# A twelve-layer network on one core: passes of two products, zeros, gathers and products of ones

## The chip, the cores and the metric

The kernel runs on one core of a Trainium2 chip. The core has a matrix engine (TensorE, PE in the profile), VectorE (DVE), ScalarE (ACT), GpSimd (POOL) and SyncE (SP), which share an on-chip memory of 128 partitions; PE writes its results to eight banks of PSUM. The metric is the device time of one execution in microseconds (us).

## The reference

`x` is 2 x 512 tokens of 256 features. Twelve sublayers are added to it, each on a layernorm of `x`. The change touches the expert layers (`_L2_ffn_ref`, two of them), the attention between them (`_L2_attn_ref`) and the waits around the last three (`_L3_ffn_ref` on both sides of `_L3_attn_ref`).

```
# L2 attention: 16 heads of 16 features, causal, each batch on its own
q, k, v = split_heads(x @ Wq.T + bq), split_heads(x @ Wk.T + bk), split_heads(x @ Wv.T + bv)
attn = softmax(where(causal, -inf, einsum('bhqd,bhkd->bhqk', q, k) * scale))
ctx  = einsum('bhqk,bhkd->bhqd', attn, v)
return ctx.reshape(b, t, D) @ Wo.T + bo

# L2 experts: 8 experts of 176 hidden features, two per token, and a shared one of 352
topk_scores, topk_idx = top_k(softmax(x @ Wr.T), 2)
out_e = einsum('bsef,edf->bsed', silu(x @ Wg[e].T) * (x @ Wu[e].T), Wd)
return sum over the two chosen experts(out_e * score) + shared

# L3 ffn: x @ (weights of -1, 0 or 1).T + bias
```

## The kernel before, in words

The work is cut into 24 units: unit u is sublayer u // 2 on batch u % 2. Each engine runs its own list of instructions and waits on semaphores where it needs another. Units 12 and 13 are the first expert layer, 14 and 15 the attention (16 heads each), 16 and 17 the second expert layer, 18 and 19 an L3 ffn, 20 and 21 the L3 attention, 22 and 23 the last ffn.

**Passes.** Values are float32. A factor is split into a high part, rounded to what one pass of PE takes (fp32r), and a low part, the rest. `mm3` (L291 to L293) makes a product of two split factors from three passes: high x high, high x low, low x high. `mm3c` does so for each chunk of 128 rows of the sum. In the profile L291, L292 and L293 are these three passes wherever `mm3` is called.

**Expert tiles** (`pe_moe2`, `act_moe2`, `dve_moe2`). GpSimd scatters the tokens to DRAM by expert. They come back in tiles of 128 tokens, 15 per batch, so 30 per layer, each with one expert whose place in `m_a` (high) and `m_b` (low) is read into a register (`value_load`, L946). PE works on three tiles at once. Round n of its loop: transpose the tokens of tile n + 1 (`tile_x`, L877), multiply tile n by the gate and up weights (`tile_gu`, six passes of 352 columns), transpose the hidden values of tile n - 1 (`tile_h`, L896), and multiply tile n - 2 by the down weights (`tile_down`, 256 columns). The 176 hidden features are a chunk of 128 and one of 48. For the second, VectorE writes the 48 features twice (L1182, at rows 0 and 64 of the chunk). Rows 64 to 127 then take the low part (L1192) and rows 0 to 63 the high part, and the down weights also stand twice in `m_a`. So one full pass (L908) does high x high and low x high, and a second pass on 64 rows (L909) high x low: five passes with the three of the first chunk. ScalarE writes x high, silu, hidden high and the result y; VectorE x low (L1170), hidden (L1177, L1182) and hidden low (L1190, L1192). SP loads token tiles and stores y tiles.

In unit 12's layer VectorE also clears `drh` and `drl` for the attention, one memset (L1234) in each of six tiles. When a batch's 15 tiles are stored, GpSimd gathers the rows of every token (L1267, eight gathers into four buffers; gathers five to eight wait until a buffer has been added), and VectorE adds them to `x` (`dve_combine`, L1060), two gathers per tile from the fourth tile of the second batch on, then takes the stats of the next unit's layernorm, one block per tile from the eighth.

**Attention 14, 15** (`pe_att2` and others). In round h PE does the scores of head h + 1, the value product of head h - 1 (`context`), and the transposes of the probabilities of head h (`pe_transpose_p`, ten blocks, L1884). VectorE takes the row minimum (L1845), ScalarE the exponential (L1853), GpSimd divides (L1871); after the transposes ScalarE writes the high part (L1900) and VectorE the low part (L1908), in three fills. The value product has 128 output rows that several heads share, each head with its columns in a matrix that is otherwise zero. Here a head takes 32 of them: 16 for the high and 16 for the low part of V. Two passes (L1996, L1998) then do it, probabilities high and low. Four groups of four heads follow one another; each group needs a split of V (L2048, L2093) and at its end a split of the result z (L2072, L2077). The output product sums over four groups: 4 x 4 x 3 = 48 passes. The second half of its weights comes by a DMA of its own (`sp_wo2`) and is split by GpSimd (`pool_wo2`) in unit 12.

**Tail.** `pe_ffn3` is nearly empty for unit 18 (its product, L1629, is issued from the expert loop) and does 16 passes each in units 22 and 23. `pe_warm` (L457) issues products of a matrix of ones, 512 columns each, whose result nobody reads; some other units have it already.

Of the kernel before, what the change touches and what calls it, by code (L numbers as in the profile page):

```python
# [24 lines left out]
ALU = mybir.AluOpType  # L25
ACT = mybir.ActivationFunctionType
AX_X = mybir.AxisListType.X
F32 = mybir.dt.float32
# [26 lines left out]
HF = P // 2  # L55
# [20 lines left out]
for _kind, _what in ORDER:  # L76
# [9 lines left out]
    else:  # L86
# [23 lines left out]
          "f3_bias": ("l_a", 2), "f3_out": ("l_qb", 2), "a2_wo_in": ("lin_in", 48), "a2_wo_hi": ("l_kvmm", 8),  # L110
          "a2_wo_lo": ("l_rope", 32)}
VG = 4
VG_N = H // VG
VS = P + 2 * HD2
V_ZERO = 4096
WO_AT = 4096


def build(nc, a, out, stop=N_UNITS):

    with ExitStack() as ctx:
# [24 lines left out]
        with ExitStack() as alias:  # L146
            a2_z2 = alias.enter_context(nc.sbuf_tensor("a2_z2", [P, NB, 2, T], F32R))
# [11 lines left out]
        with ExitStack() as alias:  # L159
            a2_sq = alias.enter_context(nc.sbuf_tensor("a2_sq", [P, 2, T], F32R))  # L160
            a2_z3 = alias.enter_context(nc.sbuf_tensor("a2_z3", [P, 2, T], F32R))
# [10 lines left out]
        with ExitStack() as alias:  # L172
            wo_raw = alias.enter_context(nc.sbuf_tensor("wo_raw", [P, H * D + 2 * D], F32))
# [17 lines left out]
        def sublayer_tensors(**shapes):  # L191
# [77 lines left out]
            lin_qh=([P, DC, T], F32R), lin_ql=([P, DC, T], F32R))  # L269
        (a2_qh, a2_ql, a2_kh, a2_kl, a2_vf, a2_sk, a2_pth, a2_ptl, a2_p) = sublayer_tensors(  # L270
# [543 lines left out]
        def pe_moe2(pe, u):  # L814
# [84 lines left out]
            def tile_down(n, at):  # L899
# [8 lines left out]
                pe.matmul(o, tail, m_a[:, bass.ds(at + (2 * DC * FE + D), D)], start=False, stop=False, skip_group_check=True)  # L908
                pe.matmul(o, tail[0:HF], m_b[0:HF, bass.ds(at + (2 * DC * FE + D), D)], start=False, stop=True,  # L909
                          skip_group_check=True).then_inc(sem("t_down"), 1)  # L910
# [156 lines left out]
        def dve_moe2(v, u):  # L1067
# [105 lines left out]
            def h(n):  # L1173
# [3 lines left out]
                v.tensor_tensor(m_h[:, n % 2, 0:P], m_ts[:, n % 2, 0:P], ps[:, 4 + n % 2, FE:FE + P], ALU.mult)  # L1177

                def twice(t):
                    return t.rearrange("p (o n) -> p o n", o=1).to_broadcast([P, 2, FE - P])  # L1180

                v.tensor_tensor(m_h[:, n % 2, P:2 * P].rearrange("p (o n) -> p o n", o=2)[:, :, 0:FE - P],  # L1182
                                twice(m_ts[:, n % 2, P:FE]), twice(ps[:, 4 + n % 2, FE + P:2 * FE]), ALU.mult)\
                    .then_inc(sem("t_h"), 1)

            def h_lo(n):
# [3 lines left out]
                v.tensor_tensor(m_hTl[:, n % 2, 0:P], ps[:, 6 + n % 2, 0:P], f32(m_hTh[:, n % 2, 0:P]), ALU.subtract)  # L1190
                low = m_hTh[HF:P, n % 2, P:2 * P]
                v.tensor_tensor(low, ps[HF:P, 6 + n % 2, P:2 * P], f32(low), ALU.subtract).then_inc(sem("t_hlo"), 1)  # L1192

# [25 lines left out]
            for n in range(n0 - 1, n0 + N2 + 1):  # L1219
# [12 lines left out]
                if m == 0 and 6 <= n - n0 < 12:  # L1232
                    k = n - n0 - 6
                    v.memset(f32((drh, drl)[k % 2][:, (k // 2) * 1408:min((k // 2 + 1) * 1408, V_ZERO)]), 0.0)\  # L1234
                        .then_inc(sem("a2_vzero"), 1)
# [35 lines left out]
        def pool_moe2(g, u):  # L1271
# [4 lines left out]
            if m == 0:  # L1276
                pool_wo2(g)
# [356 lines left out]
        def pe_ffn3(pe, u):  # L1634
            if u == 18:
                pe_T(pe, 20)
            if u >= 22:
# [294 lines left out]
        def a2_z(b, g):  # L1932

            if g < 2:
                return xh[:, b, g, :], xl[:, b, g, :]
# [1061 lines left out]
```

## Time and profile before

| | |
|---|---|
| timed runs (3) | median 1251.0 us, 1250.42 to 1256.68 |
| profiled execution | 1242.25 us, span 1240.4 us |
| PE busy | 1108.8 us (89%) |
| DVE, ACT, POOL busy | 853.0, 617.6, 543.9 us |
| granted TensorE clock, mean | 0.966 of full speed |
| chain that ended last | PE 52%, DVE 19%, ACT 6% |

The profiled execution is one run. Busy time counts what an engine executes; a wait for another engine is idle time, and the profile names what ended it. The granted clock is 1.00 at 2.4 GHz and 0.50 at 1.2 GHz. A product's time in the timeline includes its way through the engine, so the distance between two starts tells what it costs in a sequence.

### The profile page before, as it was taken

Reading aid. Unit: us, or ns where it says so; the run is one execution under the profiler, and the core shown is the slowest. Engines: PE = TensorE matmul, PEld = TensorE weight load, DVE = VectorE, ACT = ScalarE, POOL = GpSimd, SP = SyncE. Lnnn points to the kernel's source line nnn. Section 1 sums busy time; section 2 is a strip of 40 time slices with the busy share of each in tenths; the row PEclk is TensorE's granted clock in tenths of the full one; section 3 lists DMA queues with packets and bytes.
Section 4 is the critical chain, followed back from the end, with each engine's and each line's share of the span. In section 5 each row is a group of like instructions: output and inputs, shape, how many; then the busy total and the mean of one; then the engine's idle time right before and its main releaser. Section 6 shows DMA issues by size and latency. Waiting matters only on the chain.

```text
span 1240.4 us, 21764 instructions
## 1 busy us (share of the span) xinstructions
PE 1108.8 (89%) x6538; PEld 918.7 (74%) x6538; DVE 853.0 (69%) x2406; ACT 617.6 (50%) x1440; POOL 543.9 (44%) x658
## 2 busy tenths in 40 slices
PE   5887688999899999987888899996799998999996
PEld 4776357777667878865666577885699997899995
DVE  4577766778978767758868866675766655665666
ACT  2455834321114345557748856554455553555552
POOL 5576718741445450235424417223354442544430
PEclk9898999999899999999899999997999998999998
DMA  5225322230013033422102163343011110010101
GB/s 174 65 65 192 112 79 77 86 106 20 1 42 144 9 107 104 128 65 56 38 16 50 40 229 108 115 121 101 26 43 34 40 36 26 26 52 25 51 0 34
DMA packets 48611, 88.12 MB, mean 71 GB/s; under 512 B 9680, under 2 KB 28496, under 8 KB 48080
## 3 DMA queue, kind: packets, MB, share of 16 engines
q1 hardware_dynamic: 42544, 75.41, 19.2%
q0 software_dynamic: 3968, 8.85, 2.4%
q10 hardware_dynamic: 2016, 2.83, 0.7%
q8 instruction: 43, 0.70, 0.2%
q14 instruction: 40, 0.33, 0.1%
HBM read 61.50 MB, written 19.27 MB: 65 GB/s over the span
## 4 chain that ended last, share of the span: by engine, by line
PE 52%; DVE 19%; ACT 6%; issue 4%; POOL 2%; DMA 1%; SPq 0%; DVEq 0%; POOLq 0%; ACTq 0%
PE ps L291 15%; PE ps L292 14%; PE ps L293 14%; DVE a_ptl L1908 4%; PE ps L1884 4%; DVE a_p L1845 2%; ACT a_p L1853 2%; DVE x L1607 1%; PE ps L877 1%; ACT a_pth L1900 1%; PE ps L909 1%; PE ps L427 1%; DVE stats L337 1%; DVE x L1060 1%; DMA raw<-moe_y,m_pos 1%
## 5 line engine op out<-in xcount | busy, mean ns | idle before, releaser
L1871 POOL TENSOR_SCALAR a_p<-a_p,small 128x128 f32<-128x128 f32 (+3 forms) x256 | 131.8, 532 | 224.0 <-DVE small L1862 223.8
L1853 ACT ACTIVATE a_p<-a_p,small 128x128 f32<-128x128 f32 (+3 forms) x256 | 141.6, 554 | 77.4 <-DVE small L1845 76.4
L1908 DVE TENSOR_TENSOR a_ptl<-ps,a_pth 128x384 fp32r<-128x384 f32 (+1 forms) x192 | 106.5, 595 | 56.7 <-ACT a_pth L1900 56.6
L291 PE MATMUL ps<-xh,wh 128*128 128x512 f32 x304 | 126.0, 414 | 10.2 <-POOL wl L526 5.8
L292 PE MATMUL ps<-xl,wh 128*128 128x512 f32 x304 | 122.4, 403 | 0.0
L293 PE MATMUL ps<-xh,wl 128*128 128x512 f32 x304 | 122.0, 401 | 0.0
L1900 ACT ACTIVATE a_pth<-ps 128x384 fp32r<-128x384 f32 (+1 forms) x192 | 90.3, 522 | 57.1 <-PE ps L1884 56.7
L1845 DVE CUSTOM_DVE_ANT_0 a_p<-ps,maskrow 128x128 f32<-128x128 f32 (+3 forms) x256 | 111.9, 483 | 4.5 <-PE ps L293 2.6
L403 POOL TENSOR_TENSOR rstd<-veps,nhalf 128x4 f32<-128x4 f32 x24 | 26.0, 1084 | 182.6 <-DVE veps L347 182.6
L1884 PE MATMUL ps<-ident,a_p 128*128 128x128 f32 x640 | 88.3, 287 | 7.9 <-DVE a_kl L1908 3.8
L495 POOL TENSOR_TENSOR wl<-raw,wh 128x256 fp32r<-128x256 f32 (+1 forms) x64 | 88.6, 1384 | 5.3
L1884 PEld LDWEIGHTS ps<-ident,a_p 128*128 128x128 f32 x640 | 75.0, 148 | 11.5 <-DVE a_kl L1908 4.3
L493 POOL TENSOR_SCALAR wh<-raw 128x256 fp32r<-128x256 f32 (+1 forms) x64 | 45.2, 706 | 77.1 <-PE ps L293 76.7
L291 PEld LDWEIGHTS ps<-xh,wh 128*128 128x128 f32 x304 | 58.6, 193 | 25.5 <-POOL wl L526 7.7
L291 PE MATMUL ps<-m_a,xh 128*128 x180 | 66.1, 367 | 6.6 <-DVE xl L1170 4.0
L293 PEld LDWEIGHTS ps<-xh,wl 128*128 128x128 f32 x304 | 58.5, 192 | 14.6
L1607 DVE SCALAR_TENSOR_TENSOR x<-ps,small,x 128x256 f32<-128x256 f32 x128 | 61.7, 482 | 8.6 <-PE ps L293 2.2
L292 PEld LDWEIGHTS ps<-xl,wh 128*128 128x128 f32 x304 | 58.7, 193 | 10.8
L291 PE MATMUL ps<-drh,xh 128*128 (+2 forms) x160 | 60.9, 381 | 1.6 <-DVE x L1607 1.6
L292 PE MATMUL ps<-drl,xh 128*128 (+2 forms) x160 | 59.7, 373 | 0.0
L293 PE MATMUL ps<-drh,xl 128*128 (+2 forms) x160 | 59.7, 373 | 0.0
L1267 POOL DMA_INDIRECT raw<-moe_y,m_pos x24 | 23.8, 991 | 74.2 <-DMA moe_y<-m_y 65.1
(393 smaller groups left out, 3412.2 us busy)
## 6 DMA issues: line engine op xcount, KB each, us to landing
raw<-in_w SPq DMA_DIRECT2D x32, 384.0 KB, 3.1
raw<-in_qk SPq DMA_DIRECT2D x16, 512.0 KB, 3.5
raw<-moe_x SPq DMA_DIRECT2D x60, 128.0 KB, 2.2
moe_y<-m_y SPq DMA_DIRECT2D x60, 128.0 KB, 1.7
m_raw<-in_ex SPq DMA_DIRECT2D x8, 608.0 KB, 7.5
m_a<-in_ex SPq DMA_DIRECT2D x8, 608.0 KB, 5.3
raw<-in_v SPq DMA_DIRECT2D x16, 256.0 KB, 2.6
moe_x<-drh SPq DMA_DIRECT2D x8, 480.0 KB, 5.8
```

The costliest lines, as they stand in the source:

```text
L291: pe.matmul(o, l[0], r[0], start=start, stop=False, skip_group_check=True)
L292: pe.matmul(o, l[0], r[1], start=False, stop=False, skip_group_check=True)
L293: return pe.matmul(o, l[1], r[0], start=False, stop=stop, skip_group_check=True)
L493: g.tensor_scalar(oh, raw[:, p, at:n], 1.0, 1.0, ALU.mult, ALU.mult).then_inc(sem("w_hi"), 1)
L495: g.tensor_tensor(ol, raw[:, p, at:n], f32(oh), ALU.subtract).then_inc(sem("w_split"), 1)
L1607: v.scalar_tensor_tensor(out=xt, in0=ps[:, 2 + t, e * D:(e + 1) * D], scalar=w_moe1[:, t, 2 * k + e:2 * k + e + 1], in1=xt, op0=ALU.mult, ...
L1845: v.tensor_tensor_reduce(p[:, par, P_AT[i]:P_AT[i + 1]], ps[:, bank, at:at + KEYS[i]], maskrow[:, T - KEYS[i]:T], 1.0, -NEG, ALU.add, ALU.min,
L1853: s.activation(p[:, par, P_AT[i]:P_AT[i + 1]], p[:, par, P_AT[i]:P_AT[i + 1]], ACT.Exp, bias=h_nmx[:, par, i:i + 1], scale=scale, accum_ou ...
L1871: g.tensor_scalar(pp, pp, h_inv[:, par, i:i + 1], 1.0, ALU.mult, ALU.mult).then_inc(sem("at_norm"), 1)
L1884: last = pe.transpose(ps[:, banks[f], at:at + P], p[:, par, P_AT[i] + kb * P:P_AT[i] + (kb + 1) * P], ident[:, :])
L1900: s.activation(dst, ps[:, bank, 0:cols], func, **how).then_inc(sem("at_fhi"), 1)
L1908: ins = v.tensor_tensor(dst, ps[:, bank, 0:cols], f32(hi), ALU.subtract)
```

## The change

- `tile_down` calls `mm3c` over both chunks: six passes of 128 rows. VectorE writes hidden in one instruction of 176 columns and hidden low in one of 256, and the down weights stand once.
- Each head has 16 output rows, V high and V low are two matrices, and `context` calls `pe_pv`: three passes per block. Two groups of eight heads; V is split in four instructions of 128 columns per group on each engine; z is split twice; the output product sums over two chunks, 24 passes, and waits for both splits of z. `sp_wo2` and `pool_wo2` are gone.
- The zeros for V are written by GpSimd, six memsets of 1536 columns after the scatters of unit 13.
- The combine starts at the fifth tile of the second batch instead of the fourth, the stats at the ninth with two blocks per tile.
- Products of ones: 8 and 13 before the transposes of unit 20, 6 after them; 11 in the first head of unit 20, after the first fill of transposes; 8 before the transposes of unit 23, 6 before its product.

```diff
@@ pe_moe2, tile_down
-                o, tail = ps[:, n % 2, 0:D], m_hTh[:, n % 2, P:2 * P]
-                mm3(pe, o, [t[:, n % 2, 0:P] for t in (m_hTh, m_hTl)],
-                    [t[:, bass.ds(at + 2 * DC * FE, D)] for t in (m_a, m_b)], True, False)
-                pe.matmul(o, tail, m_a[:, bass.ds(at + (2 * DC * FE + D), D)], start=False, stop=False, ...)
-                pe.matmul(o, tail[0:HF], m_b[0:HF, bass.ds(at + (2 * DC * FE + D), D)], start=False, stop=True, ...)
+                mm3c(pe, ps[:, n % 2, 0:D],
+                     [[t[:, n % 2, c * P:(c + 1) * P] for t in (m_hTh, m_hTl)] for c in range(2)],
+                     [[t[:, bass.ds(at + (2 * DC * FE + c * D), D)] for t in (m_a, m_b)] for c in range(2)])
@@ dve_moe2
-                v.tensor_tensor(m_h[:, n % 2, 0:P], m_ts[:, n % 2, 0:P], ps[:, 4 + n % 2, FE:FE + P], ALU.mult)
-                v.tensor_tensor(m_h[:, n % 2, P:2 * P] ..., twice(...), twice(...), ALU.mult)
+                v.tensor_tensor(m_h[:, n % 2, 0:FE], m_ts[:, n % 2, :], ps[:, 4 + n % 2, FE:2 * FE], ALU.mult)
...
-                if m == 0 and 6 <= n - n0 < 12:
-                    k = n - n0 - 6
-                    v.memset(f32((drh, drl)[k % 2][:, (k // 2) * 1408:min((k // 2 + 1) * 1408, V_ZERO)]), 0.0)
-                if 4 <= late < 4 + TT:
-                    dve_combine(v, u, late - 4)
-                if 8 <= late < 8 + TT:
-                    dve_stats(v, u + 2, (late - 8,))
+                if 5 <= late < 5 + TT:
+                    dve_combine(v, u, late - 5)
+                if 9 <= late < 11:
+                    dve_stats(v, u + 2, (2 * late - 18, 2 * late - 17))
@@ pool_moe2
-                pool_wo2(g)
+                for k in range(6):
+                    g.memset(f32((drh, drl)[k % 2][:, (k // 2) * 1536:(k // 2 + 1) * 1536]), 0.0)
@@ pe_ffn3
             if u == 18:
+                pe_warm(pe, 8, 3)
+                pe.wait_ge(sem("x_res0"), 4 * 10)
+                pe_warm(pe, 13, 3)
                 pe_T(pe, 20)
+                pe_warm(pe, 6, 3)
             if u >= 22:
+                if u == 23:
+                    pe_warm(pe, 6, 3)
                 pe_ready(pe, u)
                 units_done(pe, u)
                 pe_scale3(pe, u)
+                if u == 22:
+                    pe_warm(pe, 8, 3)
                 pe_T(pe, u + 1)
@@ pe_transpose_p (warm is 11 in the first head of unit 20, else 0)
+                if warm and f == 1:
+                    pe_warm(pe, warm, 7)
@@ pe_att2, context
-                    pe.matmul(o, a2_v(kb, h), a2_pth[:, r], ...)
-                    last = pe.matmul(o, a2_v(kb, h), a2_ptl[:, r], ...)
+                pe_pv(pe, ps[:, 6 + h // 8, :], f0 + 4 + 3 * h, lambda kb: a2_v(kb, h % 8), a2_pth, a2_ptl,
+                      h % 8 == 0, h % 8 == 7).then_inc(sem("a2_pv"), 1)
@@ pe_att2, end of a unit
-            (48 passes over four groups; the first groups before the last z split)
+            pe.wait_ge(sem("a2_zlo"), 2 * (b + 1))
+            for t in range(TT):
+                last = mm3c(pe, acc(t), [xTt(b, c, t) for c in range(DC)], [rc(1536 + c * D, D) for c in range(DC)])
@@ act_att2 (dve_att2 likewise, with z and v_lo)
-                if h == 1:
-                    v_hi(1)
-                if h in (5, 9, 13):
-                    act_z(s, b, (h - 5) // VG_N)
-                if h in (5, 9):
-                    v_hi((h - 5) // VG_N + 2)
+                if h == 8:
+                    act_z(s, b, 0)
+                    v_hi(1)
```

## Rows read from the trace of the kernel before

**Rows 1.** Window in units 16, 17: us, busy of PE, PEld, DVE, ACT, POOL, clock, DMA.

```profile
765.00:845.00 80.00, 76.76 (x485) 65.87 (x484) 54.63 (x190) 43.52 (x126) 25.86 (x21) 1.00 0.39 121
```

**Rows 2.** Timeline of one expert tile: start us, duration us, engine, line, operation, operands.

```profile
786.30 0.36 PE L291 MATMUL ps<-m_a,xh 128*128 x1
...
786.62 0.28 PE L293 MATMUL ps<-m_a,xl 128*128 x1
...
786.74 0.28 PE L908 MATMUL ps<-m_a,xh 128*128 x1
...
786.95 0.18 PEld L909 LDWEIGHTS ps<-m_b,xh 64*128 64x128 f32 x1
...
787.26 0.44 PE L877 MATMUL ps<-ident,raw 128*128 128x128 f32 x2
...
788.65 0.36 PE L291 MATMUL ps<-m_a,xh 128*128 x1
```

**Rows 3.** The value load of the tiles, by source line: duration min/median/max in ns.

```profile
L946 PEldq TENSOR_LOAD <-m_tab x60: 297/306/547, 454.7 to 832.4; - x60
```

**Rows 4.** Timeline where a down product has no value load behind it.

```profile
841.19 0.38 PE L909 MATMUL ps<-m_b,xh 64*128 x1
...
841.50 0.39 PE L1629 MATMUL ps<-qt,xh 128*128 128x256 f32 x1
```

**Rows 5.** Timeline of a tile of unit 12 with a memset; idle time in brackets.

```profile
481.01 0.42 PE L291 MATMUL ps<-m_a,xh 128*128 x1 [0.30 <-DVE xl L1170]
...
482.10 1.23 DVE L1234 MEMSET drl<- 128x1408 f32 x1 [0.36 <-issue]
...
483.92 0.42 PE L291 MATMUL ps<-m_a,xh 128*128 x1 [0.30 <-DVE xl L1170]
```

**Rows 6.** Chain of waits from 665 to 680 us, its shares by line.

```profile
by line: DVE a_ptl L1908 42.6%; DVE a_p L1845 23.3%; ACT a_p L1853 10.9%; ACT a_pth L1900 8.1%; DVE xl L2077 4.6%; issue 4.6%; DVE small L1862 4.3%; ACT xh L2072 3.3%; DVE drh L2093 2.2%; DVE small L1845 0.8%
```

**Rows 7.** Timeline of a plain head of unit 15.

```profile
671.48 1.28 PE L1884 MATMUL ps<-ident,a_p 128*128 128x128 f32 x10
...
672.14 0.60 ACT L1900 ACTIVATE a_pth<-ps 128x512 fp32r<-128x512 f32 x1
...
675.16 0.19 PEld L1996 LDWEIGHTS ps<-a_pth,drl 128*128 128x128 f32 x1 [0.17 <-DVE a_ptl L1908]
...
675.68 1.28 PE L1884 MATMUL ps<-ident,a_p 128*128 128x128 f32 x10
```

**Rows 8.** Window inside unit 14.

```profile
585.00:590.00 5.00, 5.00 (x18) 3.93 (x17) 4.35 (x17) 4.15 (x13) 2.05 (x4) 0.50 0.07 15
```

**Rows 9.** Windows around equal products of the tail at either clock.

```profile
854.41:859.70 5.29, 5.29 (x12) 3.80 (x12) 0.69 (x1) 0.60 (x1) 3.65 (x4) 0.50 0.37 103
...
866.17:868.99 2.82, 2.82 (x14) 1.99 (x12) 2.57 (x7) 1.20 (x2) 2.11 (x4) 1.00 0.00 0
...
1226.08:1228.07 1.99, 1.99 (x16) 1.94 (x16) 1.96 (x11) 0.00 (x0) 0.12 (x1) 1.00 0.00 0
...
1233.36:1236.91 3.55, 3.55 (x16) 3.45 (x16) 1.83 (x6) 0.00 (x0) 0.00 (x0) 0.50 0.25 85
```

**Rows 10.** Timeline of GpSimd: a memset at the start, the first gather of unit 12.

```profile
0.95 0.90 POOL L2688 MEMSET drh<- 128x960 f32 x1
...
501.12 1.06 POOL L1267 DMA_INDIRECT raw<-moe_y,m_pos  x1 [39.83 <-DMA moe_y<-m_y]
```

**Rows 11.** Timeline of VectorE: the last combine of unit 12's rows.

```profile
515.87 0.48 DVE L1060 SCALAR_TENSOR_TENSOR x<-raw,small,x 128x256 f32<-128x256 f32 x1 [1.37 <-DMA raw<-moe_y,m_pos]
```

**Rows 12.** Value split (L2093) and z split (L2077) by source line.

```profile
L2093 DVE TENSOR_TENSOR drh<-a_vf,drh x4: 414/420/424, 547.4 to 677.5; 128x256 fp32r<-128x256 f32 x4
...
L2077 DVE TENSOR_TENSOR xl<-ps,xh x4: 690/691/692, 579.8 to 695.1; 128x512 fp32r<-128x512 f32 x4
```

**Rows 13.** Window of unit 15's output product, 48 products long.

```profile
726.94:732.65 5.71, 5.71 (x51) 5.71 (x50) 3.98 (x9) 1.00 (x3) 0.00 (x0) 1.00 0.89 326
```

**Rows 14.** Timeline of a group of products of ones.

```profile
646.63 1.25 PE L461 MATMUL ps<-onesb 128*128 128x512 bf16 x5
```

More of the change, by code:

```diff
@@ L54 @@
 SH_CH = -(-FS // P)
-HF = P // 2
 EW = 2 * DC * FE + 2 * D
@@ L904, in tile_down @@
                     pe.wait_ge(*since("t_y", n - 1))
-                o, tail = ps[:, n % 2, 0:D], m_hTh[:, n % 2, P:2 * P]
-                mm3(pe, o, [t[:, n % 2, 0:P] for t in (m_hTh, m_hTl)],
-                    [t[:, bass.ds(at + 2 * DC * FE, D)] for t in (m_a, m_b)], True, False)
-                pe.matmul(o, tail, m_a[:, bass.ds(at + (2 * DC * FE + D), D)], start=False, stop=False, skip_group_check=True)
-                pe.matmul(o, tail[0:HF], m_b[0:HF, bass.ds(at + (2 * DC * FE + D), D)], start=False, stop=True,
-                          skip_group_check=True).then_inc(sem("t_down"), 1)
+                mm3c(pe, ps[:, n % 2, 0:D],
+                     [[t[:, n % 2, c * P:(c + 1) * P] for t in (m_hTh, m_hTl)] for c in range(2)],
+                     [[t[:, bass.ds(at + (2 * DC * FE + c * D), D)] for t in (m_a, m_b)] for c in range(2)])\
+                    .then_inc(sem("t_down"), 1)
             if m == 0:
@@ L1276, in pool_moe2 @@
             if m == 0:
-                pool_wo2(g)
+                for k in range(6):
+                    g.memset(f32((drh, drl)[k % 2][:, (k // 2) * 1536:(k // 2 + 1) * 1536]), 0.0).then_inc(sem("a2_vzero"), 1)
             if m == 1:
@@ L1986, in context @@
             def context(h):
[L1987 to L2000 removed]
+                if h % 8 == 0:
+                    pe.wait_ge(sem("a2_vlo"), TT * (2 * b + h // 8 + 1))
+                pe_pv(pe, ps[:, 6 + h // 8, :], f0 + 4 + 3 * h, lambda kb: a2_v(kb, h % 8), a2_pth, a2_ptl,
+                      h % 8 == 0, h % 8 == 7).then_inc(sem("a2_pv"), 1)
             for h in range(H):
@@ L2044, in v_hi @@
             def v_hi(g):
-                s.wait_ge(sem("a2_vf"), TT * (b + 1))
-                if g >= 2:
-                    s.wait_ge(sem("a2_pv"), H * b + VG_N * (g - 1))
-                s.activation(a2_vslot(g, 0), a2_vsrc(g), ACT.Copy).then_inc(sem("a2_vhi"), 1)
+                for t in range(TT):
+                    s.wait_ge(sem("a2_vf"), 4 * b + t + 1)
+                    s.activation(a2_vslot(True, t), a2_vf[:, t, g * P:(g + 1) * P].rearrange("p (h n) -> p h n", h=8),
+                                 ACT.Copy).then_inc(sem("a2_vhi"), 1)
             v_hi(0)
@@ L2091, in v_lo @@
             def v_lo(g):
-                v.wait_ge(sem("a2_vhi"), VG * b + g + 1)
-                v.tensor_tensor(a2_vslot(g, 1), a2_vsrc(g), f32(a2_vslot(g, 0)), ALU.subtract).then_inc(sem("a2_vlo"), 1)
+                for t in range(TT):
+                    v.wait_ge(sem("a2_vhi"), TT * (2 * b + g) + t + 1)
+                    v.tensor_tensor(a2_vslot(False, t), a2_vf[:, t, g * P:(g + 1) * P].rearrange("p (h n) -> p h n", h=8),
+                                    f32(a2_vslot(True, t)), ALU.subtract).then_inc(sem("a2_vlo"), 1)
             v.wait_ge(sem("a2_vzero"), 6)
@@ L2262, in pair @@
                     pe_transpose_p(pe, n + hh, hh, a3_p, [bank["p", hh, f] for f in range(3)],
-                                   [starts["p", hh, f] for f in range(3)])
+                                   [starts["p", hh, f] for f in range(3)], 11 if side and first and hh == 0 else 0)
                     if side and first and hh == 1:
@@ L2778, in _ @@
                 sp_expert(sp, e)
-            sp_wo2(sp)
             sp_moe2(sp, 12)
```

119 lines of the change are left out of this document (23 added, 96 removed).

## Prediction

> **What bounds the kernel now.** I read the windows by stage first, then the timeline of single steps, and last the chain of waits inside the attention heads. Four places are touched.
>
> The expert tiles (units 12/13 and 16/17, 30 tiles each) are bound by TensorE: it is busy 76.8 of 80 us, clock granted in full [rows 1]. One tile repeats every 2.35 us (786.30 to 788.65 in [rows 2]) with no idle time of PE in it. Inside it the full-size 256-column products follow one another at 0.12 us (786.62 to 786.74), but the last pair does not: the product on 64 rows (L909) begins its weight load only at 786.95, 0.21 us after L908 began, and the transpose after it begins another 0.31 us later. So L908 and L909 take 0.52 us. Is it the value load between two tiles (L946, 0.31 us on PE's sequencer, [rows 3]) that holds the transpose? At 841.19 the same product is followed by work with no load before it, and again the next product starts 0.31 us later [rows 4]. The 64-row form itself stops the overlap of one product with the next load, on both sides.
>
> Six tiles of unit 12 carry a memset of 1.23 us on VectorE. There the low half of x is late and PE idles 0.30 us; the tile takes 2.91 us (481.01 to 483.92) [rows 5].
>
> The 16-wide attention (units 14, 15) is not bound by PE. The chain from 665 to 680 us holds DVE and ACT lines and no PE line at all [rows 6]. A plain head repeats at 4.20 us (transposes at 671.48 and 675.68, [rows 7]). But PE has little slack: its transposes start at 671.48, and ACT empties their first bank at 672.14 without having been idle before it: the two arrive together. Where the clock is at half, PE is the bound instead: 5.00 of 5 us busy at 585 [rows 8].
>
> The tail (845 to 877, and 1228 on) is a chain of small steps with TensorE at half clock after its idle stretches: twelve 512-column products take 5.29 us at 854 and 2.82 at 866; sixteen 256-column ones 3.55 us at 1233 and 1.99 at 1226 [rows 9].
>
> **The change, part by part.**
>
> *Six passes in the down product.* L908 and L909 (0.52 us) become three full products, 3 x 0.115 = 0.35. That is 0.175 us less per tile, 10.5 over 60. DVE does one product and one subtraction fewer per tile, ACT as much as before; PE waits for neither in [rows 2], and I take it that their lead is longer than 0.175. What is late next is PE's sequencer, which walks value load, address steps and waits for every tile; its load then starts nearer to its use. I keep both ends: nothing gained (0), and 0.2 per tile (12).
>
> Here the Trainium skill gives two rules that pull apart. TensorE: Matmul & The Clock Gate, "Why this matters for your kernels", says that a single product with few rows takes as long as a full one; then six passes instead of five would cost 60 x 0.115 = 7 us more, not 10.5 less. TensorEngine Tiling (Array Packing), "Key Properties", says that a change of the tiling mode drains the engine; [rows 2, 4] side with it, with 0.21 and 0.31 us where 0.12 is usual.
>
> *Zeros by GpSimd.* The six DVE memsets go: 6 x (2.91 - 2.35) = 3.4 us. GpSimd writes 6 x 1536 columns instead; 960 columns took it 0.90 us [rows 10], so about 1.4 each, 9 in all. It stands idle 39.83 us before its gather at 501 [rows 10], and the zeros are wanted at 540: hidden. Without that cover it would be 9 us. The removed weight load and split of the old layout sat in the same idle time: 0.
>
> *Gathers one tile later.* In unit 12's rows the combine waits 1.37 us for its eighth gather [rows 11]. But gathers five to eight are issued only as the first combines free their buffers, so they move later as well, and the tiles between get shorter. A wait at the first gathers goes, one at the last grows. I take 0 (2.5 gained to 2 lost); two stats in one tile fit into the time DVE gains.
>
> Expert tiles: 10.5 + 3.4 = 14 us less.
>
> *Three passes in the value product.* Per head one more product for each of 512, 384, 256 and 128 columns: 1280 columns, 0.59 us at the 2.82 us for twelve times 512 [rows 9]. The 512-column one fits into the wait of PE for DVE's second fill. The last three come after DVE's fills and delay the transposes: the third 384-column product takes the 0.17 us idle gap before 675.16 [rows 7], the 256- and 128-column ones add 0.11 + 0.06. So the transposes start 0.17 us later. In a plain head this goes straight onto ACT (no slack); where DVE also does stats, norms or a combine it has about 0.2 us of cover. 10 plain heads x 0.17, some 14 others at 0.05, and the last head of each unit, where PE is the path, 2 x 0.45: 3.3 us. Ends: 0, and 32 x 0.59 = 19.
>
> *Value split and z.* Per unit DVE did four v splits (0.42) and four z splits (0.69) [rows 12]; now eight v splits of half the columns (I take 0.28, between half of 0.42 and all of it) and two z. That is 4.4 against 3.6 us, gathered in head 8 instead of heads 1, 5, 9 and 13: 0.7 less per unit, 1.4.
>
> *Output product.* 48 products took 5.71 us [rows 13]; 24 take 2.86. They now all wait for z: ACT's copy, then DVE's split of 0.69 [rows 12], beside eight transposes. I estimate that at 0.8 us after the first product's old start: 2.0 less per unit, 4.1 in both. QK of unit 15 and the router of unit 16 follow directly.
>
> *Clock in the heads.* Stretches at half clock like that at 585 [rows 8] follow heads in which PE waits long for z and v splits; busier heads should lose some. I take 1 us (0 to 4; one in head 8 may come).
>
> Attention: -3.3 + 1.4 + 4.1 + 1 = 3.2 us less.
>
> *Products of ones.* Five took 1.25 us, 0.25 each, the first ones included [rows 14]; I take 0.21, which is twice the 256-column step. After unit 17, 8 + 13 take 4.5 to 5.3 us in a wait that lasts until 851, so they delay nothing, and the clock should stay: 5.29 becomes 2.82 (2.5), transposes of unit 20 some 0.7, and the later half-clock stretch at 874, covered by 11 products, 0.8. The 11 delay a transpose that DVE's combine hides. I take 3.5 of these 4. At the end, 8 + 6 in the waits of unit 23: 3.55 becomes 1.99, 1.5. Ends: 0 and 6 for both; if they don't fit their waits, 2 lost.
>
> Sum: 14 + 3.2 + 3.5 + 1.5 = 22 us. The profiled execution took 1242.25 us (span 1240.4), so 1220 for it. The median of the timed runs is 1251.0, 0.7% above it; I take 21 from that: **1230 us**. Its own range is 1220 to 1240.
>
> **Rivals.**
>
> A, PE's sequencer takes over in the tiles. For: the load (0.31 us, [rows 3]) and the address steps of each tile sit there, and two more instructions join. Against: at 841 the gap was the same without a load. The 10.5 are gone: 1240.5.
>
> B, the third pass lands on the path in every head. For: ACT's start ties with PE's transposes; half clock doubles it. Against: no PE line in the chain. 19 in place of 3.3: 1246.
>
> C, slower: passes count, whatever their rows. One mechanism, TensorE's work in both loops: six passes cost 7 where I gain 10.5 (17.5 worse), and B's 15.7 comes with it, 1230 + 33 = 1263. It decides if the tile period in the new trace is above 2.35 us. The Trainium skill's rule on few rows (TensorE: Matmul & The Clock Gate, "Why this matters for your kernels") would be its first part. Against it stand [rows 2, 4].
>
> D, the clock falls all the same between products of ones: 5 less gained, 1235.
>
> **Numbers.** My forecast 0.60, A 0.13, B 0.12, C 0.07, D 0.08. Within 0.5% (6.3 us, what a measurement tells from no change) is 1244.7 to 1257.3. Faster: 0.60 + 0.08 + 0.12 of A + 0.03 of B, less 0.02 for runs that scatter by some us: 0.81. Same: the rest of A and B and that 0.02, 0.12. Slower: C, 0.07. Range 1216 to 1245: the forecast's own, D, A, and the near part of B; below it, four more us for gains nearer to their upper ends.
>
> **What would show it.** Period of a tile 2.17 us and down products in six steps of 0.115; 2.3 or more means A, above 2.35 C. No tile of 2.9 us in unit 12. Plain heads at 4.2 to 4.4 us; at 4.7 B holds. Head 8 near 6 us, heads 5, 9, 13 shorter. Out-products of 2.9 us after z. Full clock at 854 and 1233. Wrong would be: a longer wait for the eighth gather, more than 2 us, or half clock in more than four places of the heads.

## The result, and the profile after it

The changed kernel takes 1235.74 us (median of 3 runs, 1233.43 to 1239.07) against 1251.0: ratio 0.9873 (95% interval 0.9841 to 0.9906), 15.9 us less at the ratio. Forecast were 1230 (ratio 0.983) and a range from 1216 to 1245. In five more rounds it gave 0.9879 (0.9859 to 0.9899).

The forecast rests on one profile of the kernel before; a second profile of each kernel stands beside the first here. This table cuts each span at the first and last value load of the tiles (30 per stretch) and at the first transposes of each head (us; "best" is a version that comes below):

```
stretch                        before  before(2)  after  after(2)  best
start to the first tile         454.7    455.6    461.1   456.3    457.5
tiles of units 12, 13            70.3     74.0     68.6    68.5     65.3
to unit 14's first head          27.7     27.3     25.4    25.6     27.1
heads 0 to 15 of unit 14         75.4     77.4     73.3    73.1     71.1
output product, next q and k     25.9     25.4     24.9    24.8     24.4
heads 0 to 15 of unit 15         68.6     67.6     70.3    70.3     66.2
to unit 16's first tile          42.0     42.8     41.3    41.3     40.7
tiles of units 16, 17            67.7     70.5     69.2    68.9     66.4
to unit 20's first head          36.8     36.4     32.7    32.8     32.8
heads of units 20, 21           350.5    350.4    351.2   351.0    351.2
end                              20.8     20.8     19.2    19.2     19.2
span                           1240.4   1248.2   1237.2  1231.8   1222.0
```

Two things stand out. The tail (up to unit 20's first head, and the end) gains about what was forecast. The tiles and unit 15 don't, and the first column differs from the second by 8 us though the kernel is the same; that comes last.

A tile, in the timeline of the changed kernel (start, duration, engine, line, operation, operands); it answers to [rows 2]:

```profile
788.70 0.42 PE L283 MATMUL ps<-m_a,xh 128*128 x1
...
789.96 0.36 PE L283 MATMUL ps<-m_a,xh 128*128 x1
...
790.16 0.28 PE L284 MATMUL ps<-m_b,xh 128*128 x1
790.28 0.28 PE L285 MATMUL ps<-m_a,xl 128*128 x1
...
790.63 0.28 PE L285 MATMUL ps<-m_a,xl 128*128 x1
790.75 0.38 PE L869 MATMUL ps<-ident,raw 128*128 128x128 f32 x2
790.93 0.42 PE L283 MATMUL ps<-m_a,xh 128*128 x1
```

The six down products run from 789.96 to 790.75 in steps of 0.12 (the first takes 0.20, as before). The gaps of 0.21 and 0.31 are gone. But from gate and up (788.70) to the next gate and up (790.93) it is 2.23 us; the median over the tiles is 2.235, not 2.17.

A plain head of unit 15, which answers to [rows 7]:

```profile
674.48 0.44 PE L283 MATMUL ps<-a_pth,drh 128*128 128x384 f32 x1 [0.21 <-DVE a_ptl L1898]
674.76 0.34 PE L284 MATMUL ps<-a_ptl,drh 128*128 128x384 f32 x1
674.94 0.33 PE L285 MATMUL ps<-a_pth,drl 128*128 128x384 f32 x1
675.11 0.28 PE L283 MATMUL ps<-a_pth,drh 128*128 128x256 f32 x1
...
675.75 1.28 PE L1874 MATMUL ps<-ident,a_p 128*128 128x128 f32 x10
...
676.41 0.60 ACT L1890 ACTIVATE a_pth<-ps 128x512 fp32r<-128x512 f32 x1 [0.30 <-PE ps L1874]
...
680.23 1.28 PE L1874 MATMUL ps<-ident,a_p 128*128 128x128 f32 x10
```

One head takes 4.48 us (675.75 to 680.23), before 4.20. ScalarE's fill now waits 0.30 us for PE's transposes, which it did not. The chain of waits from 673 to 683 says the same. Where [rows 6] held no PE line, PE has 38% of it:

```profile
by line: DVE a_ptl L1898 35.0%; DVE a_p L1833 15.7%; PE ps L283 12.3%; ACT a_pth L1890 12.2%; PE ps L1874 9.5%; PE ps L285 8.2%; PE ps L284 8.2%; DVE small L1850 4.9%; issue 2.0%; DVE small L1833 0.5%
```

The tail, by windows with the columns of [rows 9]: the twelve 512-column products before unit 20's heads, and a stretch of products of ones:

```profile
854.12:857.02 2.90, 2.90 (x12) 2.17 (x12) 0.57 (x1) 0.60 (x1) 2.29 (x3) 1.00 0.40 120
846.90:848.90 2.00, 2.00 (x11) 0.92 (x10) 1.83 (x4) 0.63 (x1) 1.76 (x1) 1.00 0.01 2
```

The granted clock is 1.00 in both windows, the full level (2.4 GHz), and what took 5.29 us at 0.50 takes 2.90. In the timeline of the end sixteen products that took 3.55 us take 1.96 (1231.70 to 1233.54 and one more step), behind two groups of ones:

```profile
1226.39 1.90 PE L453 MATMUL ps<-onesb 128*128 128x512 bf16 x8
...
1229.76 1.46 PE L453 MATMUL ps<-onesb 128*128 128x512 bf16 x6
...
1231.70 0.36 PE L1609 MATMUL ps<-qt,xh 128*128 128x256 f32 x1 [0.48 <-DVE xl L447]
...
1233.54 0.28 PE L1609 MATMUL ps<-qt,xl 128*128 128x256 f32 x1
```

### The profile page after: what moved, and what is told of

It reads as the page before. It is cut to its first block, busy times and chain, and to the rows that moved or that the text cites. A ratio compares the mean times of both kernels' runs of the same rounds, so it can differ in the third digit from the quotient of the medians.

```text
span 1237.2 us, 22024 instructions
## 1 busy us (share of the span) xinstructions
PE 1122.8 (91%) x6730; PEld 940.8 (76%) x6730; DVE 832.0 (67%) x2284; ACT 614.5 (50%) x1444; POOL 550.8 (45%) x662
## 4 chain that ended last, share of the span: by engine, by line
PE 54%; DVE 19%; ACT 6%; issue 4%; POOL 2%; another core or an unknown queue 0%; SPq 0%; DMA 0%; DVEq 0%; POOLq 0%; ACTq 0%
PE ps L283 16%; PE ps L285 15%; PE ps L284 15%; DVE a_ptl L1898 4%; PE ps L1874 3%; DVE a_p L1833 2%; ACT a_pth L1890 2%; ACT a_p L1841 2%; PE ps L869 1%; DVE x L1587 1%; PE ps L888 1%; DVE stats L329 1%; DVE x L1050 1%; PE ps L1609 1%; PE ps L419 1%
## 5 line engine op out<-in xcount | busy, mean ns | idle before, releaser
L1874 PE MATMUL ps<-ident,a_p 128*128 128x128 f32 x640 | 84.9, 280 | 5.0 <-DVE a_kl L1898 2.1
L283 PE MATMUL ps<-m_a,xh 128*128 x240 | 83.2, 347 | 4.1 <-DVE xl L1174 2.3
L1874 PEld LDWEIGHTS ps<-ident,a_p 128*128 128x128 f32 x640 | 72.5, 144 | 8.1 <-DVE a_kl L1898 2.6
L284 PE MATMUL ps<-m_b,xh 128*128 x240 | 72.7, 303 | 0.0
L285 PE MATMUL ps<-m_a,xl 128*128 x240 | 72.5, 302 | 0.0
L284 PEld LDWEIGHTS ps<-xl,wh 128*128 128x128 f32 x304 | 58.1, 191 | 10.6
```

The lines of the kernel that those rows point to most:

```text
L283: pe.matmul(o, l[0], r[0], start=start, stop=False, skip_group_check=True)
L284: pe.matmul(o, l[0], r[1], start=False, stop=False, skip_group_check=True)
L285: return pe.matmul(o, l[1], r[0], start=False, stop=stop, skip_group_check=True)
L1874: last = pe.transpose(ps[:, banks[f], at:at + P], p[:, par, P_AT[i] + kb * P:P_AT[i] + (kb + 1) * P], ident[:, :])
```

## Experiments

Ratios are to the kernel before, in runs on the same chip, with 95% intervals. "On record" is the prediction above.

**again**: the changed kernel, no edit.

> The changed kernel once more, unchanged. In its first trace four tiles in each stretch around the gathers take 3 to 4.5 us, because ScalarE's Silu starts 2.3 to 3.3 us after the product that it waits for has ended, and the untouched part ahead of the tiles took 6 us longer than in the kernel before. Theory E (these late starts belong to one execution): the ratio of medians stays at 0.987, and in this profile the late starts are gone or stand elsewhere; tiles of over 2.8 us change their places. Theory G (they come with the gathers that now fall one tile later): the same tiles are long again, some 9 us in all. Either way the median tile takes 2.235 us, and a plain head 4.49.

Measured 0.9879; span 1231.9, of which the untouched part ahead of the tiles took 4.8 us less than in the first profile. The long tiles are there again, at the same tiles (4.37, 4.01, 3.63, 4.11 and 4.08 us among them, from value load to value load). Theory E, that they change their places, fell, and G looked right. But b_six, b_attn and b_ones, whose gathers are not shifted, have such tiles at their gathers too (3.2 to 6.2 us), so it isn't the shift.

**b_six**: the six passes alone.

```
-                v.tensor_tensor(m_hTl[:, n % 2, 0:P], ps[:, 6 + n % 2, 0:P], ...)
-                v.tensor_tensor(low, ps[HF:P, 6 + n % 2, P:2 * P], f32(low), ALU.subtract)
+                v.tensor_tensor(m_hTl[:, n % 2, :], ps[:, 6 + n % 2, 0:D], ...)
...
-                mm3(pe, o, ...); pe.matmul(o, tail, m_a...); pe.matmul(o, tail[0:HF], m_b[0:HF, ...])
+                mm3c(pe, ps[:, n % 2, 0:D], ...)
```

> The kernel before with the six full passes of the down product alone. My forecast on record: period of a tile 2.17, 10.5 us less, ratio 0.992. Theory Q (PE's sequencer is nearly full at this pace: value load, address steps and waits of one tile take it 2.2 us): period 2.23 to 2.24, 60 x 0.11 = 6.7 us less, ratio 0.9947; where the value load takes 0.5 instead of 0.3 us, that tile is 0.1 to 0.2 longer. Rival C (passes count, whatever their rows): 7 us more, ratio 1.006.

Measured 0.9915 (0.9886 to 0.9945), 10.6 us less: the number of the forecast, not for its reason. The median tile takes 2.24 us, so the period is worth 60 x 0.11 = 6.6. The rest is most likely VectorE's: it now does two operations fewer per tile (one product and one subtraction where there were two of each), and in this profile that alone hides the memsets. b_full5 below, which relieves TensorE but not VectorE, supports it. Its timeline, to be held against [rows 5]:

```profile
481.39 0.43 PE L290 MATMUL ps<-m_a,xh 128*128 x1
...
481.85 1.23 DVE L1224 MEMSET drh<- 128x1408 f32 x1 [0.24 <-issue]
...
483.54 0.42 PE L290 MATMUL ps<-m_a,xh 128*128 x1
```

The tile with the same memset of 1.23 us lasts 2.15 us, not 2.91, and no tile with a memset is over 2.3. (In the kernel before, the memsets made five tiles long, 2.77 to 2.91 us, and a sixth 2.42: 2.6 us in all, not 6 x 0.56.)

**b_zero**: zeros by GpSimd, combines and stats one tile later.

```
-                if m == 0 and 6 <= n - n0 < 12:
-                    v.memset(f32((drh, drl)[k % 2][:, (k // 2) * 1408:...]), 0.0)
-                if 4 <= late < 4 + TT:
-                    dve_combine(v, u, late - 4)
+                if 5 <= late < 5 + TT:
+                    dve_combine(v, u, late - 5)
...
+                for k in range(6):
+                    g.memset(f32((drh, drl)[k % 2][:, (k // 2) * 1408:...]), 0.0)
```

> The kernel before with the zeros written by GpSimd and with the combines and stats one tile later, nothing else. My forecast on record: the six tiles of 2.91 us take 2.35, 3.4 us less, the gathers 0: ratio 0.997. Theory H (the zeros are hidden, the later gathers give 2 more): 5 us less, 0.996. Rival I (under held semaphores the memsets were hidden in part, or the last gather is now later): 0 to 1 less, ratio 0.999 to 1.000.

Measured 0.9997 (0.9972 to 1.0022), the number of rival I, but not for its reasons: the memsets weren't hidden before, as the second profile of the kernel before has the same five long tiles, and VectorE no longer waits for a gather in unit 12's rows. The six tiles take 2.35 us as forecast. From the first tile to unit 14's first head this profile takes 97.9 us, against 98.0 and 101.3 in the two of the kernel before. The timed runs show no gain; the forecast's 3.4 us stand at the end of the interval. Where the gain of the six tiles went wasn't measured, and the zeros and the later combines were not run apart.

**b_attn**: the new attention alone.

```
-                    pe.matmul(o, a2_v(kb, h), a2_pth[:, r], ...)
-                    last = pe.matmul(o, a2_v(kb, h), a2_ptl[:, r], ...)
+                pe_pv(pe, ps[:, 6 + h // 8, :], f0 + 4 + 3 * h, lambda kb: a2_v(kb, h % 8), a2_pth, a2_ptl, ...)
...
-                    v.memset(f32((drh, drl)[k % 2][:, (k // 2) * 1408:min((k // 2 + 1) * 1408, V_ZERO)]), 0.0)
+                    v.memset(f32((drh, drl)[k % 2][:, (k // 2) * 1536:(k // 2 + 1) * 1536]), 0.0)
```

> The kernel before with the new attention of units 14 and 15 alone (three passes, two groups, output product in 24 products); the zeros are written by VectorE in the old places. My forecast on record: 3.2 us less, ratio 0.9974, plain head 4.37. Theory P (PE is now on the path of each plain head: all three products of the second fill and of the last two blocks wait for VectorE's fill): plain head 4.49, that is 0.29 longer, some 20 of them; this eats most of the gain in heads 5, 9, 13 and in the output product: 0 to 2 us less, ratio 0.9985 to 1.000. Rival B: plain head 4.7 or more, 10 us and more slower, ratio 1.008.

Measured 1.0021 (0.9999 to 1.0044): 2.6 us more where 3.2 less was forecast. Plain heads take 4.49 to 4.50, as theory P says. One part of the loss isn't the attention's: the memsets, still VectorE's, now write 1536 columns instead of 1408, and the six tiles that hold them exceed 2.35 by 3.7 us in sum, before by 2.6.

**b_ones**: the products of ones alone.

```
             if u == 18:
+                pe_warm(pe, 8, 3)
+                pe.wait_ge(sem("x_res0"), 4 * 10)
+                pe_warm(pe, 13, 3)
                 pe_T(pe, 20)
+                pe_warm(pe, 6, 3)
...
+                if u == 22:
+                    pe_warm(pe, 8, 3)
                 pe_T(pe, u + 1)
...
(and 11 in the first head of unit 20, as in the changed kernel)
```

> The kernel before with the products of ones alone, those inside unit 20's first head included. My forecast on record: 5.0 us less, ratio 0.996: 3.5 between the last tile and unit 20's first transposes, 1.5 at the end. Rival D (the clock falls all the same between them): no change, ratio 1.000.

Measured 0.9950 (0.9927 to 0.9974), 6.3 us less. Rival D falls. In this profile the stretch up to unit 20's first head takes 34.0 us against 36.8 and 36.4.

**a_no3**: the changed kernel without the product of low v and high p.

```
-        last = mm3(pe, o[:, kb * P:T], v(kb), (pth[:, r], ptl[:, r]), ...)
+        pe.matmul(o[:, kb * P:T], a2_v(kb, h % 8)[0], a2_pth[:, r], ...)
+        last = pe.matmul(o[:, kb * P:T], a2_v(kb, h % 8)[0], a2_ptl[:, r], ...)
```

> The changed kernel without the third value product (low v times high p) of units 14 and 15: two products a block, the rest of the new attention kept; the third term is left out of the result. Theory P: plain head 4.20 as before the change, 6 to 8 us less than the changed kernel, ratio 0.982; the output product, head 8 and the shorter heads 5, 9, 13 show what the rest of the new attention gives: 6 to 8 us less than the kernel before over the two units. Rival (the third product is mostly hidden, the longer plain head has another cause): 4.4 or more, ratio 0.986 to 0.988.

Measured 0.9796 (0.9765 to 0.9827); 10.4 us below the changed kernel, with plain heads of 4.20 again. The heads of units 14 and 15 take 72.2 and 66.0 and the output stretch 23.2, together 7 us less than in the changed kernel. So the third product costs 7 us by the traces and 10.4 by the times (whose two intervals leave some 4.6 either way): two to three times the 3.3 of the forecast. Without it the new attention does gain.

**a_order**: the changed kernel, third product kept, with another order and finer waits.

```
-                    pe.wait_ge(sem("at_flo"), fill + kb + 1)
-                last = mm3(...)                       # vh*ph, vh*pl, vl*ph of one block
+                pe.wait_ge(sem("at_fhi"), fill + 1)   # ScalarE's fill
+                products(0, False)                    # vh*ph, vl*ph
+                pe.wait_ge(sem("at_flo"), fill + 1)   # VectorE's fill
+                products(0, True)                     # vh*pl
+                pe.wait_ge(sem("at_fhi"), fill + 3)
+                for kb in (1, 2, 3):
+                    products(kb, False)
+                pe.wait_ge(sem("at_flo"), fill + 2)
+                products(1, True)
+                pe.wait_ge(sem("at_flo"), fill + 3)
+                products(2, True)
+                products(3, True)
```

> The changed kernel with the three value products of a block in another order and with finer waits: the two that read ScalarE's fill (high v and low v) wait for ScalarE alone, and only the one that reads VectorE's fill waits for VectorE. Theory P (PE is on the path of a plain head because nine products wait for VectorE's second and third fill, which ends 0.85 us before the transposes): now three small ones are left after it, the transposes start early enough, plain head 4.20 again, some 20 heads by 0.29 and the busy ones by a part of it: 6 to 8 us less than the changed kernel, ratio to before 0.982. Rival J (ScalarE or VectorE lose as much by PE's earlier start, since the path ties them all): head 4.4 or more, ratio 0.986 to 0.988. Rival K (PE waits more in one piece, and its clock falls in more places): heads shorter, sum the same.

Measured 0.9800 (0.9769 to 0.9830), 9.9 us below the changed kernel, and the same as a_no3, which has two products. Its plain heads take 4.08, less than the 4.20 there; its two heads 14 take 4.40, more than the 4.16. A head in its timeline (L1956 holds all value products):

```profile
663.57 0.28 PE L1956 MATMUL ps<-a_pth,drh 128*128 128x256 f32 x1
...
663.87 0.27 PE L1956 MATMUL ps<-a_pth,drl 128*128 128x128 f32 x1
...
663.98 0.57 PE L1956 MATMUL ps<-a_ptl,drh 128*128 128x384 f32 x3
...
664.39 1.27 PE L1874 MATMUL ps<-ident,a_p 128*128 128x128 f32 x10
```

VectorE's two fills end at 663.97 (1.02 from 662.95). The transposes begin 0.42 us later, with three products between them; in the changed kernel it was 0.85 (674.90 to 675.75) with seven.

**a_waits**: the changed kernel with three waits of PE per tile left out that an earlier wait of PE implies.

```
-                if n >= 2:
+                if n >= 2 and n < n0 + 2:
                     pe.wait_ge(*since("t_xlo", n - 1))
...
-                if n >= 2:
+                if n >= 2 and n < n0 + 2:
                     pe.wait_ge(*since("t_h", n - 1))
...
-                else:
-                    pe.wait_ge(*since("t_hlo", n - 1))
```

> The changed kernel without three waits of PE in each tile that an earlier wait of PE for the same or a higher count implies (x low half before the transposes of x, h before gate and up, h low half before the transposes of h). Each takes PE's sequencer 0.106 us. Theory Q (the sequencer is nearly full in a tile): period 2.17 instead of 2.235, and tiles in which the value load takes 0.5 us are no longer than the others: 3 to 5 us less than the changed kernel, ratio to before 0.984. Rival L (the array sets the period): 2.23 as before, ratio 0.988.

Measured 0.9818 (0.9788 to 0.9849), 7.6 us below the changed kernel; tiles of 2.114 us, and 60 x 0.12 = 7.3. No work of the array was taken away, so TensorE's sequencer had a part in the pace. Which part, the value loads tell (duration min/median/max in ns; the changed kernel, then a_waits; it answers to [rows 3]):

```profile
L936 PEldq TENSOR_LOAD <-m_tab x60: 296/363/613, 461.1 to 834.1; - x60
...
L934 PEldq TENSOR_LOAD <-m_tab x60: 296/302/520, 459.6 to 826.6; - x60
```

In the changed kernel the next load begins 2.12 us after one that took under 0.33 us (20 tiles, median, those over 2.6 left out) and 2.31 us after one of over 0.44 (19 tiles): a long load goes straight into the tile. In the kernel before the two are 2.34 and 2.31: there it is covered. In a_waits 44 of 49 such tiles have a short load, at 2.11 us. So the three waits, some 0.33 us of the sequencer's time, gave 0.12 per tile, about what the long loads cost; at 2.11 something else holds the tile, and TensorE's products are the likely limit. The same work in its timeline:

```profile
784.24 0.38 PE L869 MATMUL ps<-ident,raw 128*128 128x128 f32 x2
784.37 0.41 PE L283 MATMUL ps<-m_a,xh 128*128 x1
...
785.41 0.38 PE L886 MATMUL ps<-ident,m_h 128*128 128x128 f32 x2
785.54 0.36 PE L283 MATMUL ps<-m_a,xh 128*128 x1
...
786.35 0.38 PE L869 MATMUL ps<-ident,raw 128*128 128x128 f32 x2
```

From the x transposes to gate and up it is 0.13 us; in the changed kernel 0.18 to 0.22.

**b_full5**: the kernel before, its 64-row product over 128 rows.

```
-                pe.matmul(o, tail[0:HF], m_b[0:HF, ...], ...)
+                pe.matmul(o, tail, m_b[:, ...], ...)
```

> The kernel before with its product on 64 rows taken over all 128 rows, as the others (the result then holds terms that don't belong). It tells whether the 0.52 us of the last two down products come from the 64-row form. Theory on record (the form stops the overlap on both sides): down products in five steps, 0.957 less (0.21 + 0.31 - 2 x 0.12) = 0.68 us; the tile is then bound by PE's sequencer at 2.13 to 2.2 instead of 2.347, ratio 0.990 to 0.993. Rival R (the gap of 0.31 before the transposes is the sequencer's, behind the value load, or a product with few rows takes as long as a full one and no more): 0.957 and 2.347 stay, ratio 1.000.

Measured 0.9971 (0.9947 to 0.9995). The median tile takes 2.21 us; the product follows its neighbour in 0.12:

```profile
791.33 0.28 PE L293 MATMUL ps<-m_a,xl 128*128 x1
...
791.45 0.28 PE L908 MATMUL ps<-m_a,xh 128*128 x1
...
791.57 0.28 PE L909 MATMUL ps<-m_b,xh 128*128 x1
...
791.77 0.41 PE L877 MATMUL ps<-ident,raw 128*128 128x128 f32 x2
```

So the 64-row form did cost the first gap (0.21 to 0.12), and the value load did not. The second gap, 0.31 us, is 0.20 here and 0.12 with six products: it was the form's too, but with five products the tile meets another limit at 2.2 us before it is all gained. Five full products are worth hardly more than six (2.21 against 2.235), which fits a limit outside the array. The timed gain is a third of b_six's. VectorE keeps its extra operations, and the memset tiles stay at up to 2.9 us and those with combines at 2.6 to 2.7.

**before_again**: the kernel before, no edit.

> The kernel before once more, unchanged, for a second profile. In the profiles of after, again, b_six, b_attn and b_ones (among them kernels whose tiles are untouched) increments of semaphores arrive 1 to 7 us after the instruction that makes them has ended, only while GpSimd issues a series of indirect DMAs; the profile of the kernel before has none of these, and its 1242 us lie 9 us below the median of its timed runs. Theory E (an undisturbed execution was profiled by luck, the kernel mostly runs with them): this profile has late increments, its tiles of unit 12 take some 75 us instead of 70.3 and those of unit 16 some 70 to 73 instead of 67.7, the time is 1248 to 1254. Rival F (the edits bring them): none, 1242.

Measured 1249.89 us. Its timeline after the gathers of unit 12 begin:

```profile
506.39 0.95 POOL L1267 DMA_INDIRECT raw<-moe_y,m_pos  x1 [0.31 <-issue]
...
506.87 0.33 PE L293 MATMUL ps<-m_a,xl 128*128 x1
...
507.64 0.95 POOL L1267 DMA_INDIRECT raw<-moe_y,m_pos  x1 [0.30 <-issue]
...
509.46 0.32 ACT L998 ACTIVATE m_ts<-ps 128x176 f32<-128x176 f32 x1 [2.49 <-remote]
```

The last gate and up product ends at 507.20, and the Silu that needs it starts at 509.46, 0.87 us after GpSimd's last issue of the group ends. Theory E holds: the unedited kernel has the late starts too, so the edits don't bring them. Its first profile is the only one of the 14 on record here without them, so they are probably usual; the runs that were only timed can't tell.

**b_direct**: the gathers as plain DMAs.

```
-                g.indirect_dma_start(out=..., in_=ys[b][:, :], in_offset=bass.IndirectOffsetOnAxis(...))
+                g.dma_start(..., ys[b][c * P:(c + 1) * P, :])
```

> The kernel before with the 32 gathers of units 12, 13, 16 and 17 as plain DMAs of the same bytes from the same queue (rows are then not those that belong; the scatters stay indirect). Theory V (increments of semaphores are held while GpSimd issues a series of indirect DMAs, whatever the other engines do): the late increments at 506 to 516 and 818 to 824 are gone, those around the scatters (444 to 462, 758 to 772) stay; tile stretches some 2 to 4 us shorter each, ratio 0.994 to 0.998. Rival W (they come from the traffic of the tiles' own loads and stores): they stay, ratio 1.000.

Measured 0.9940 (0.9916 to 0.9964), 7.5 us less. Theory V holds as far as it was tested: no late increment (a semaphore update that comes late, see the last section) around the tiles' gathers, and those around the scatters (at 446 to 464 and 760 to 778) and at 130 to 146 stay. The two tile stretches take 72.3 and 68.3 us against 74.0 and 70.5, which is 3.9 of the 7.5; plain DMAs may also save time in other ways, and that wasn't told apart. GpSimd's four issues look like this:

```profile
509.53 2.28 POOL L1267 DMA_DIRECT2D raw<-moe_y  x4 [43.17 <-DMA moe_y<-m_y]
```

**a_best**: the changed kernel with both edits, a_order and a_waits.

> The changed kernel with both edits of the last runs, the order of the value products and the three waits less. If they act in different places, as theories P and Q say, the ratios multiply: plain head 4.08, tile 2.11, ratio to before 0.9800 x 0.9818 / 0.9879 = 0.974, some 1218 us. Rival M (a shorter tile puts more of the held semaphores and of the gathers onto the path, or the clock falls more): 0.978 or more.

Measured 0.9749 (0.9717 to 0.9780), 1220.21 us: below the kernel before by 2.5% and below the changed kernel by 1.3%. The product of the two edits' ratios, 0.974, lies within the interval. Tiles take 2.114, plain heads 4.08. Of M a little is seen: one half-clock stretch at 683 makes head 8 of unit 15 take 6.70 us, 5.71 in a_order, and the two tile stretches sum to 131.7 us against 130.0 in a_waits.

## Why the forecast was right, and where it was not

The sign, the range and the tail were right, and 1230 missed by 5.7 us. The parts measured alone (10.6 + 0.4 - 2.6 + 6.3 = 14.7 us) sum to the 15.9 of the whole within their intervals, so each can be held against its term: the tiles gave 11.0 where 14 was forecast, the attention -2.6 where 3.2 was, the ones 6.3 where 5 was. Two terms were wrong in size and one of those in sign; the range was wide enough for it.

- **Six passes, term 10.5.** The reading of [rows 2, 4] was right: with full rows the two gaps go (b_six; in b_full5 the second falls to 0.20). The down products shrank from 0.957 to 0.803 us, 0.154 of the forecast 0.175. The failed step is "against: at 841 the gap was the same without a load", by which rival A was set aside. A had named the right resource. That row only shows that the sequencer wasn't the limit *before*. Its work per tile (value load, four pairs of address steps, four waits) takes about 2.05 us with a value load of 0.30 and 2.25 with one of 0.5 (the sum of the steps in the trace of the changed kernel), which was covered at 2.35 and is not at 2.17. The period fell by 0.11, and a_waits gave another 0.12 by taking sequencer work alone. The Trainium skill (Perfetto Trace Analysis, "Sequencer-only Instruction (DRAIN, etc)") says that a profile shows only the execution of such an instruction, and neither its wait nor the propagation of its semaphore. This trace fits that: a wait of PE shows as 0.051 us, and the next instruction of its sequencer starts 0.106 us or more after it began.
- **Zeros, term 3.4.** Too large, and counted twice. The six tiles held 2.6 us, as not all of them took 2.91. And both this edit and the six passes relieve VectorE in them: either alone takes them to the common period (b_six, b_zero). "DVE does one product and one subtraction fewer" stood in the forecast at no gain; it was worth these 2.6 and part of the tiles with combines, and behind it the zeros have nothing left to give. Together the tiles' terms gave 11, not 14.
- **Gathers, term 0.** No run had them alone. In the changed kernel VectorE waits for no gather; the wait of [rows 11] is gone. b_zero, with the zeros, measured 0.4 us.
- **Third value product, term 3.3.** The mis-sized one: 10.4 us by the times, 7 by the traces (a_no3). In a plain head the third 384-column product was to fit into the 0.17 us gap at 675.16. It doesn't: the next product starts 0.21 us after VectorE's last fill ends, before it was 0.05. These 0.16 and 0.13 for the two small ones make 0.29 per head, not 0.17. Head by head against a_no3, 12 plain heads make 3.5 us, six heads of 4.40 with side work 0.1 each where 0.2 of cover was to hide it, and the stretch from the last head of unit 14 to the first of unit 15 1.7. A half-clock stretch at head 8 adds 1 us in unit 15 (6.80 against 5.76), but in unit 14 it is a_no3 that has one (5.76 against 6.34), so that isn't the product's doing. B's sign, heads at 4.7, was not met, but its mechanism, PE on the path, holds in the plain heads at 0.29.
- **Output product, v and z, clock, terms 4.1, 1.4 and 1.** The output product runs from 729.19 to 732.10, 2.91 us, behind a wait of 0.52 for z. Half clock shows at three places of the heads and their output, before at four. The three terms should give 6.5; in a_no3, which has them without the third product, heads and output stretch take 161.4 us against 169.9 and 170.4 in the two profiles of the kernel before. They gave more than forecast, 8.5 to 9 us; how these split among them wasn't measured.
- **Ones, term 5.** 6.3 (0.9950), and in the table 4 and 1.6 us, at the places named. (One of these steps is 0.216 us, as taken; it is less than twice the 256-column step of 0.115, which the forecast gave as its source.)
- **Carrying over.** "0.7% above it; I take 21" treated the gap of 9 us between the profile and the median as scatter. It was, at least in part, a different condition of the same kernel: the first profile had no late semaphore increments (see the last section), the second one has, and takes 6.5 us more in the tiles. The two first profiles differ by 3 us and the medians by 15. The other part of that is the untouched start, 6.4 us longer in the first profile of the changed kernel, with 51 us of it at half clock against 27 in the kernel before and 31 in the changed kernel's second profile.

Rival C fell at once (2.235 against its 2.35). Its rule from the Trainium skill (TensorE: Matmul & The Clock Gate, "Why this matters for your kernels"), that few rows cost as much as many, is one on a single product, which no run here has by itself. Between full ones the last two down products, one of them on 64 rows, took 0.52 us, where with full rows they took 0.24 to 0.32.

## What to carry to other kernels

When work leaves the busiest unit, add up the next one first, and for TensorE that is also its sequencer: in the changed kernel its 2.05 to 2.25 us per tile held a loop of products that can run at 2.11, and three waits that earlier ones imply were worth 0.12 us per tile together. Terms that relieve the same engine in the same stretch don't add. And before a third product is called expensive, ask which operand each product waits for: with the two that needed only ScalarE's half issued early, a kernel with three products took no longer than one with two in the old order (0.9800 and 0.9796). Two products in the new order were not run.

## What the runs showed that was not expected

While GpSimd issues a series of indirect DMAs, the semaphore increments of the other engines can arrive late. Taking for each instruction the next recorded increment of its semaphore, one that comes over 0.8 us after its end was found for TensorE never in the first profile of the kernel before, 36 times in its second, 43 and 37 times in the changed kernel and in b_ones; for VectorE and ScalarE 37 and 31 times in the changed kernel and never in the first profile. The traces lack some increments, so these counts are upper bounds. Nearly all lie within or just behind such a series. In the changed kernel:

```profile
507.43 0.33 PE L285 MATMUL ps<-m_a,xl 128*128 x1
...
508.59 0.94 POOL L1246 DMA_INDIRECT raw<-moe_y,m_pos  x1 [0.30 <-issue]
...
510.55 0.32 ACT L988 ACTIVATE m_ts<-ps 128x176 f32<-128x176 f32 x1 [3.28 <-PE ps L285]
```

The profile names the later product (ended 510.16) as the releaser; by the order of work it is the one at 507.43, which ended at 507.76, 2.79 us before. Replacing the 32 gathers by plain DMAs removed the late increments around them and 0.6% of the time. What decides whether an execution has them, as the first profile did not, stays open, and so does the mechanism: no run here tells a shared path for the increments from another cause.

A value load of PE's sequencer took 0.30 to 0.61 us in the changed kernel. Of 60 loads 15 were over 0.44 us in the kernel before, 21 in the changed one, 4 and 3 in a_waits and a_best. They cost time in the changed kernel, as told under a_waits; why a load is long is open.
